# Gated cross attention with a stream mixer: low parts a unit later on GpSimd, ScalarE's free work ahead of its bank copies, other units for two projections

## The reference

```python
# step 1: windowed cross attention; q and k from the normalised x, v from the context
q = Wq @ xn + bq;  k = Wk @ xn + bk;  val = Wv @ ctx + bv          # 256 x 2048 a batch
# windows of 128 columns, 8 heads of 32 rows
attn = softmax(q_h^T k_h / sqrt(32), masked);  o = gelu(attn applied to val)
x = x + tanh(g_xattn) * (Wo @ o + bo) * mask
# step 2: four streams of 512 columns, mixed row by row
xn2 = layernorm(x)
H_res = sinkhorn(50 iterations, 4 x 4 logits of each row);  H_pre, H_post = softmaxes
y = (sum_n H_pre[n] * stream_n) @ W_branch
out_i = sum_j ((1-g) I + g H_res)[i, j] * stream_j + H_post[i] * y
x = x + tanh(g_ffn) * out
```

## Time and profile before

| what | value |
|---|---|
| median of three runs | 1883.52 us (1878.68 to 1887.21) |
| profiled execution | 1878.06 us, span 1876.2 us |
| granted TensorE clock, mean | 0.884 |
| busy: TensorE, VectorE, ScalarE, GpSimd | 1423.7, 1390.8, 1055.6, 799.5 us |

### The profile page before, as it was taken

One profiled execution on the slowest core, in us unless ns is written; L12 is line 12 of the kernel. 1 busy time (PEld: TensorE's weight loads), 2 busy tenths in 40 slices (PEclk: granted clock), 3 DMA queues, 4 the chain that ended last, 5 costly groups with the idle time before them and its releaser, 6 DMA issues.

```text
span 1876.2 us, 35394 instructions
## 1 busy us (share of the span) xinstructions
PE 1423.7 (76%) x12448; PEld 859.5 (46%) x12448; DVE 1390.8 (74%) x3582; ACT 1055.6 (56%) x2017; POOL 799.5 (43%) x1333
## 2 busy tenths in 40 slices
PE   2779999888988888888888888888898886522223
PEld 1546556555645454545555454445555554220011
DVE  3334545666788897888888888888777887777777
ACT  3457776666766666665666666656666564311111
POOL 3223334555454544455354535454454534323320
PEclk9889999999989998999899898989999997755656
DMA  8457766566656665666656565665556543321123
GB/s 259 138 163 194 215 172 167 170 179 194 180 149 179 182 190 168 197 186 186 195 157 176 171 181 165 187 167 171 170 167 175 136 125 90 101 79 56 56 87 115
DMA packets 173920, 299.85 MB, mean 160 GB/s; under 512 B 23568, under 2 KB 74640, under 8 KB 169648
## 3 DMA queue, kind: packets, MB, share of 16 engines
q1 hardware_dynamic: 156336, 264.03, 45.0%
q0 software_dynamic: 17408, 33.56, 10.2%
HBM read 179.81 MB, written 67.11 MB: 132 GB/s over the span
## 4 chain that ended last, share of the span: by engine, by line
PE 43%; DVE 22%; POOL 11%; ACT 10%; issue 9%; DMA 2%; SPq 2%; DVEq 0%; POOLq 0%; ACTq 0%
PE pr L610 11%; PE pr L624 7%; PE pr L637 6%; POOL kp L536 5%; PE f L739 4%; DVE ssum L1160 4%; PE av_ps L724 4%; POOL ctx_hl L476 3%; DVE otile_odd L1207 3%; DVE negm L1034 2%; PE av_ps L728 2%; SPq L404 2%; DVE sa L1161 2%; PE s_ps L697 2%; DVE sv L1161 1%
## 5 line engine op out<-in xcount | busy, mean ns | idle before, releaser
L1160 DVE TENSOR_REDUCE ssum<-kp 128x16 f32<-128x64 f32 x768 | 181.8, 237 | 208.3 <-POOL kp L536 206.1
L536 POOL TENSOR_TENSOR kp<-ke,sa 128x64 f32<-128x64 f32 x392 | 158.0, 403 | 283.8 <-DVE sa L1161 283.8
L536 POOL TENSOR_TENSOR kp<-ke,sv 128x64 f32<-128x64 f32 x376 | 166.2, 442 | 226.7 <-DVE sv L1161 225.7
L476 POOL TENSOR_TENSOR ctx_hl<-ctx_raw,ctx_hl 128x512 bf16<-128x512 f32 x128 | 149.6, 1174 | 217.3 <-ACT ctx_hl L792 217.3
L610 PE MATMUL pr<-x_hl,wq 128*128 128x512 bf16 x768 | 205.8, 426 | 35.1 <-POOL x_hl L471 35.1
L1034 DVE TENSOR_REDUCE negm<-s_ps 128x4 bf16<-128x512 f32 x256 | 167.0, 652 | 74.7 <-PE s_ps L697 73.2
L697 PE MATMUL s_ps<-k_st,q_st 97*128 97x128 bf16 x1024 | 104.4, 226 | 151.3 <-DVE negm L1034 138.4
L610 PE MATMUL pr<-x_hl,wk 128*128 128x512 bf16 x768 | 197.4, 412 | 8.0 <-DVE logit L1100 8.0
L637 PE MATMUL pr<-o_sb,wo 128*128 128x512 bf16 x768 | 188.0, 389 | 8.8 <-POOL o_sb L482 6.6
L837 ACT ACTIVATE probs<-st_ps,key_bias 128x512 f32<-128x512 f32 x256 | 173.3, 677 | 30.0 <-PE st_ps L711 29.5
L471 POOL TENSOR_TENSOR x_hl<-xc,x_hl 128x512 bf16<-128x512 f32 x128 | 148.5, 1160 | 92.8 <-ACT x_hl L805 92.8
(11 more groups left out here) (140 smaller groups left out, 2965.0 us busy)
## 6 DMA issues: line engine op xcount, KB each, us to landing
xs<-in_dram SPq DMA_DIRECT2D x128, 256.0 KB, 4.9
xc<-in_dram SPq DMA_DIRECT2D x32, 1024.0 KB, 10.7
ctx_raw<-in_dram SPq DMA_DIRECT2D x32, 1024.0 KB, 7.0
x1c<-in_dram POOLq DMA_DIRECT2D x64, 512.0 KB, 9.3
x_dram<-x1c SPq DMA_DIRECT2D x32, 1024.0 KB, 4.7
q_st<-q_hl SPq DMA_DIRECT2D x384, 64.0 KB
k_st<-k_hl SPq DMA_DIRECT2D x384, 64.0 KB
x1t_even<-x_dram SPq DMA_DIRECT2D x16, 1024.0 KB, 5.8
```

Of the source, the lines that this page charges most:

```text
L476: ins = nc.gpsimd.tensor_tensor(ctx_hl[:, 1, t, :], ctx_raw[:, t, :], ctx_hl[:, 0, t, :], ALU.subtract)
L536: nc.gpsimd.tensor_tensor(kp[:], ke[:], v, ALU.mult).then_inc(kp_made, 1)
L1160: cf.link(nc.vector.tensor_reduce(s_t, k, AX.X, ALU.add))
```

## The change

The tables move work between the units of a chunk. Of x, the low parts move from units 2, 5, 6, 7 to 3, 5, 6, 7, while the high parts stay at 1, 4, 5, 6. Of the context, the low parts move from units 0, 1, 1, 4 to 1, 2, 2, 3, and the high parts stay at 0, 0, 1, 1. The first half of the value projection moves from unit 6 to 4, the output projection from units 4 and 5 to 5 and 6, the mixer's logits from 7 to 5, its selection from 8 to 9, and its statistics from 1 and 3 to 2 and 5. All output tiles stand one unit later (`TILE_AT` 54 for 53), the transposes of their `pre` part two units later. The second `add_x` of a chunk moves from unit 7 to unit 0 of the next, the store of the sum from unit 1 to 2.

On GpSimd the two kinds of low part change places within a unit: the context's now stands between scalings 1 and 2, x's between 2 and 3. On ScalarE the context's and x's high parts, the first product and the first of the output tiles move from behind the bank copies and the reciprocal to the place ahead of them. `spare` gets three columns, one for each use.

```diff
--- before.py
+++ after.py
@@ -53,11 +53,11 @@
 FIRST = -2 * UPC
 RING = 4
 
-HI_X_AT, LOW_X_AT = [1, 4, 5, 6], [2, 5, 6, 7]
-HI_CTX_AT, LOW_CTX_AT = [0, 0, 1, 1], [0, 1, 1, 4]
-
-T_AT, LOGITS_AT, SELECT_AT = [3, 3, 4, 4], 7, 8
-STAT_B_AT = [1, 3]
+HI_X_AT, LOW_X_AT = [1, 4, 5, 6], [3, 5, 6, 7]
+HI_CTX_AT, LOW_CTX_AT = [0, 0, 1, 1], [1, 2, 2, 3]
+
+T_AT, LOGITS_AT, SELECT_AT = [3, 3, 4, 4], 5, 9
+STAT_B_AT = [2, 5]
 
 
 STAT_AT = UPC + STAT_B_AT[1]
@@ -67,15 +67,15 @@
 SINK += [(it, it + 1) for it in range(RETURN + 1, ITERS, 2)]
 RETURN_AT = SINK_AT + SINK.index((RETURN, None))
 
-BESIDE = dict(load=-8, first=-6, xpre=-5, pre=-4, branch_0=0, branch_1=1, out_0=-1, out_1=0,
+BESIDE = dict(load=-8, first=-6, xpre=-5, pre=-3, branch_0=0, branch_1=1, out_0=-1, out_1=0,
               stream_1=0, stream_2=1, y=2, stream_3=4, pair_1=5, pair_2=6, pair_3=7, store_0=5, store_1=8)
 BEHIND = dict(load=-5, first=-3, xpre=-3, pre=-2, branch_0=-1, branch_1=-1, out_0=-1, out_1=0,
               stream_1=0, stream_2=1, y=2, stream_3=3, pair_1=3, pair_2=4, pair_3=5, store_0=4, store_1=6)
 LAST_BESIDE = B - 3
-TILE_AT = {(f, t): UNITS * (f + 1) + 53 + UPC * t for f in range(LAST_BESIDE + 1) for t in range(DT)}
+TILE_AT = {(f, t): UNITS * (f + 1) + 54 + UPC * t for f in range(LAST_BESIDE + 1) for t in range(DT)}
 TILE_AT.update({(B - 2, t): NU + SINK_AT - 1 + 6 * t for t in range(DT)})
 TILE_AT.update({(B - 1, t): NU + SINK_AT + len(SINK) + 1 + 6 * t for t in range(DT)})
-assert SINK_AT + len(SINK) < 53
+assert SINK_AT + len(SINK) < 54
 LAST = TILE_AT[B - 1, DT - 1] + UPC
 XS = DT * 4
 XSN = 4
@@ -116,7 +116,7 @@
 
     if b == 1:
         return [p - 1 for p in range(XS)]
-    return [UNITS * (b - 1) + UPC * (p // 4 - 2) + 2 * (p % 4) for p in range(XS)]
+    return [UNITS * (b - 1) + UPC * (p // 4 - 2) + (1, 3, 4, 5)[p % 4] for p in range(XS)]
 
 
 STAT_PIECES = {}
@@ -134,9 +134,9 @@
     made += [("pre", f, t) for f, t in tiles_at(g, "pre")]
     if 0 <= G + 1 < NG:
         made += {0: [("q", G + 1, 0)], 1: [("q", G + 1, 1)], 2: [("k", G + 1, 0)], 3: [("k", G + 1, 1)],
-                 6: [("v", G + 1, 0)], 7: [("v", G + 1, 1)]}.get(r, [])
-    if 0 <= G - 1 < NG and r in (4, 5):
-        made += [("o", G - 1, 2 * (r - 4)), ("o", G - 1, 2 * (r - 4) + 1)]
+                 4: [("v", G + 1, 0)], 7: [("v", G + 1, 1)]}.get(r, [])
+    if 0 <= G - 1 < NG and r in (5, 6):
+        made += [("o", G - 1, 2 * (r - 5)), ("o", G - 1, 2 * (r - 5) + 1)]
     if g == -1:
         made.append(("csum", 0, 0))
     return made
@@ -218,7 +218,7 @@
         gate_sb = sb("gate_sb", [P, 3])
         gt = sb("gt", [P, 8])
         ones = sb("ones", [P, P])
-        spare = sb("spare", [P, 1])
+        spare = sb("spare", [P, 3])
         csum = sb("csum", [P, NL])
         bn_a = sb("bn_a", [P, DT, 4, 6])
         mv_a = sb("mv_a", [P, DT, 2])
@@ -433,7 +433,7 @@
                 if r == 0 and 1 <= G + 2 < NG:
                     sp.wait_ge(x_split, DT * (G + 2))
                     load_xc(G + 2)
-                if r == 1 and 0 <= G - 2 < NG:
+                if r == 2 and 0 <= G - 2 < NG:
                     store_x1(G - 2)
                 for later in STAT_PIECES.get(g + 4, []):
                     load_xs(*later)
@@ -557,18 +557,20 @@
                     for ready in ffn_at(g, STAT_AT + 1 + part):
                         stat_b(ready, part)
                 scale_at(f, its, 1)
+                for H, t in at_step(g, -1, LOW_CTX_AT):
+                    split_ctx(H, t)
+                if 0 <= G - 1 < NG and r == 4:
+                    low_gelu(G - 1, 0)
+                scale_at(f, its, 2)
+                if 0 <= G - 1 < NG and r == 4:
+                    low_gelu(G - 1, 1)
                 for H, t in at_step(g, -2, LOW_X_AT):
                     split_x(H, t)
-                if 0 <= G - 1 < NG and r == 3:
-                    low_gelu(G - 1, 0)
-                scale_at(f, its, 2)
-                if 0 <= G - 1 < NG and r == 3:
-                    low_gelu(G - 1, 1)
-                for H, t in at_step(g, -1, LOW_CTX_AT):
-                    split_ctx(H, t)
                 scale_at(f, its, 3)
-                if 0 <= G - 1 < NG and r in (6, 7):
-                    add_x(G - 1, r - 6)
+                if 0 <= G - 1 < NG and r == 7:
+                    add_x(G - 1, 0)
+                if 0 <= G - 2 < NG and r == 0:
+                    add_x(G - 2, 1)
 
         @block.tensor
         def _(pe):
@@ -948,6 +950,17 @@
                     exp_scores(g - 1)
                 if 0 <= G - 1 < NG and r == 3:
                     hi_gelu(G - 1)
+
+                for H, t in at_step(g, -1, HI_CTX_AT):
+                    hi_ctx(H, t)
+                for H, t in at_step(g, -2, HI_X_AT):
+                    norm_x(H, t)
+                    hi_x(H, t)
+                for done, t in tiles_at(g, "first"):
+                    first_products(done, t)
+                for pair in range(2):
+                    for done, t in tiles_at(g, f"out_{pair}"):
+                        first_out(done, t, pair)
                 made = banked_at(g)
                 for n, what in enumerate(made):
                     if what[0] in "qk":
@@ -964,11 +977,6 @@
                         inverse_den(g - 2)
                 if not made and 0 <= g - 2 < NU:
                     inverse_den(g - 2)
-                for H, t in at_step(g, -1, HI_CTX_AT):
-                    hi_ctx(H, t)
-                for H, t in at_step(g, -2, HI_X_AT):
-                    norm_x(H, t)
-                    hi_x(H, t)
                 if g == FIRST + UPC + 3:
                     w_parts(2, wv, wv_loaded)
                 if g == -2:
@@ -977,11 +985,6 @@
                     gelu(G - 1)
                 if g >= 0 and u == 15 and b + 1 < B:
                     xstat(b + 1)
-                for done, t in tiles_at(g, "first"):
-                    first_products(done, t)
-                for pair in range(2):
-                    for done, t in tiles_at(g, f"out_{pair}"):
-                        first_out(done, t, pair)
                 for n in range(2):
                     for ready in ffn_at(g, STAT_AT + 1 + n):
                         inverse_roots(ready, n)
@@ -1071,7 +1074,7 @@
                     cf.link(ins)
 
             def stat_finish(f):
-                nc.vector.memset(spare[:, 0:1], 0.0)
+                nc.vector.memset(spare[:, 1:2], 0.0)
                 for t in range(DT):
                     ins = nc.vector.bn_aggr(mv_b[:, t, :], bn_b[:, t].rearrange("p j s -> p (j s)"))
                 ins.then_inc(mv_b_ready, 1)
@@ -1161,7 +1164,7 @@
                 nc.vector.reciprocal((sv if half else sa)[:], s_t).then_inc(scale_made, 1)
                 if half and it == RETURN:
                     dve.wait_ge(scale_made, HALVES * f + 2 * it)
-                    ask(nc.vector.memset(spare[:, 0:1], 0.0))
+                    ask(nc.vector.memset(spare[:, 2:3], 0.0))
                 if half and it == ITERS - 1:
                     dve.wait_ge(scale_made, HALVES * (f + 1))
                     coefficients(f)
```

## The result

| what | before | after |
|---|---|---|
| median | 1880.32 us (1877.19 to 1887.21) | 1899.14 us (1894.87 to 1901.76) |
| span of the profiled execution | 1876.2 us | 1900.0 us |
| granted clock, mean | 0.884 | 0.871 |

The ratio is 1.0103 with an interval of 1.0082 to 1.0123: the change made the kernel slower by 19 us, where 1839 was forecast, and outside the stated range of 1795 to 1890. The forecast put 0.12 on slower. (The two profiled executions differ by 23.8 us; the changed one is the slowest of its five.)

The account below looks back on a forecast made before the run. VectorE was taken to set the period, held by GpSimd's scaling. -4.5 + 1.2 + 0.6 + 0.3 = -2.4 us a chunk, -50 over 21 chunks, -45 with the tail: 1833, median 1839, range 1795 to 1890.

Parts of the forecast that it names:

- The removed term in unit 1: VectorE's 3.24 us idle for GpSimd's scaling in unit 1 goes, leaving that unit at about 6.5 us.
- The added term in unit 2: Two context low parts on GpSimd between scalings 1 and 2 make VectorE wait 1.2 us a chunk.
- All of GpSimd's terms together: VectorE's waits for scaling, a chunk: 4.05 us removed, 1.2 added in unit 2, 0.6 in units 6 and 7.
- The tail: After the attention, the last two batches' Sinkhorn iterations start one unit later: +5.2 us.
- What it moves on TensorE: Moved transposes, projections and branch products keep TensorE's sum per chunk; with 3.3 us of slack left, nothing counted.
- ScalarE's order only a price (0.3 us a chunk): ScalarE's free work ahead of q's copy and the reciprocal may wait for `xc`'s load: 0 to 0.6 us, 0.3 taken.
- Rival 1: TensorE becomes the bound through slow projections in units 3 to 7, costing VectorE 1.2 us a chunk: median 1863, chance 0.15.
- Rival 2: VectorE's additions stretch beside x's low parts on GpSimd, 2.1 us a chunk instead of 0.6: median 1870, chance 0.15.
- The sign "TensorE's wait for the maximum nearly halved and the clock higher": Listed as showing the forecast right: TensorE waits nearly half as long for VectorE's maximum, and the clock rises.
- Rival 3: `xc`'s load lands after 15.2 us, ScalarE holds q and the reciprocal, VectorE loses 4.2 us: median 1927, chance 0.12.
- Rival 4: The added waits hide and only the removed 4.5 us a chunk shows: median 1794, chance 0.13.
- The early chunks: The ten chunks before 497.8 us have few additions and no such idle time; no change counted.

Follow-up runs that it names:

- kernel 4: Kernel before with GpSimd's new order of low parts and ScalarE's new order of free work, projections and mixer units unmoved: 1819.67 us, ratio 0.9668.
- Experiment 8: Changed kernel with GpSimd waiting for the mixing coefficients, and the transposes of `pre` in unit 2 instead of 3: 1856.80 us, ratio 0.9891.
- 11: Transposes of `pre` in unit 2 instead of 3, on both orders plus moved mixer units and GpSimd's wait for the coefficients: 1873.66 us, ratio 0.9945.
- Kernel 3: Kernel before with only ScalarE's order changed, its context and x copies, first products and first output tiles ahead of the bank copies: 1809.23 us, ratio 0.9612.
- kernel 2: Kernel before with only GpSimd's part changed, the units and order of the low parts of context and x: 1836.11 us, ratio 0.9758.
- experiment 1: Changed kernel plus one wait: where a batch's iterations end, GpSimd waits until VectorE has made the mixing coefficients: 1874.05 us, ratio 0.9961.

## Why the prediction was wrong

**What was right.** The removed term in unit 1: it fell to 5.97 us, against "about 6.5". The added term in unit 2: VectorE waited 1.30 us there (1.2 taken). A timeline of the changed kernel:

```profile
1216.35 2.72 POOL L476 TENSOR_TENSOR ctx_hl<-ctx_raw,ctx_hl 128x512 bf16<-128x512 f32 x2
...
1219.36 0.22 DVE L1163 TENSOR_REDUCE ssum<-kp 128x16 f32<-128x64 f32 x1 [1.30 <-POOL kp L536]
```

All of GpSimd's terms together (-4.05 + 1.2 + 0.6 = -2.25 us a chunk) measured (43.1 - 69.1) / 12 = -2.2. That close a sum is partly luck. By units, the mean wait for the scaling fell by 2.8 us in unit 1 (3.24 forecast) but rose from 0.89 to 1.14 in unit 0, where 0.81 should have gone; it rose by 0.9 in unit 2 (1.2), which as a whole grew by 2.5 us where about 1 was expected, and by 0.3 in units 6 and 7 together (0.6), and fell by 0.5 in unit 3, where nothing was counted. The 0.4 us for the copy of q did not go: 5.1 us in three batches became 5.6, now in unit 2. The tail: from the last maximum to the end 300.4 us against 296.0, +4.4 (5.2 forecast).

**The step that failed** is "What it moves on TensorE": "The sum per chunk is the same", and "so I count nothing here either". With it fails the silence on the mixer's moved units, for which the sum has the tail alone, 5 us. The order inside a chunk has a price that a sum of work does not show. On kernel 4, the price of the projections measured 26 us (46 for the values, 20 back), that of the mixer's units 38 us and 30 more for the burst. Added to the orders' -61 (1819.67 against about 1881) this gives 1820 + 26 + 68 = 1914 us, 15 above what was measured (21 by the ratios). So the parts are not additive, as experiments 8 and 11 show too: with the mixer's units already moved, the projections cost 11 us (1899.14 against 1887.73, which also differ in one statistic). For the orders alone the measured 1820 lies in the forecast's own range, 1812 to 1863, and is more than the -45 I had for the whole. (The lower end of that range is not what its terms' ends add up to: without any added wait they give -4.5 us a chunk, not -3.6.)

**The cover I misread.** I laid the gain at the low parts' later units and gave ScalarE's order only a price (0.3 us a chunk). Kernel 3 shows the reverse: -72 us by ScalarE's order without any low part moved. The earlier trace rows held it: the copy of the context stood behind a copy of q that waited 3.75 us. Both edits act on that one place, and either shortens unit 1 (10.16 us a chunk to 7.13 in kernel 2, 6.77 in kernel 3, 6.44 with both), so their gains do not add.

**Rival 1** (TensorE the bound, 1863) came in part. TensorE was not the bound: its busy time in the stretch did not grow (529.7 to 507.1 us, with one in eighty of its records missing after), and its wait for the maximum rose. But what the rival described, little to do ahead of unit 3 and then slow work, is in the trace. Unit 2 of the chunk shown had a clock of 0.65, and in unit 3 TensorE came to k only behind its wait and two sets of transposes:

```profile
1222.68 0.61 PE L699 MATMUL s_ps<-k_st,q_st 97*128 97x128 bf16 x4 [4.09 <-DVE negm L1037]
...
1224.34 1.12 PE L659 MATMUL pr<-id_sb,x1c 128*128 128x128 f32 x4
1225.25 1.06 PE L686 MATMUL pr<-id_sb,xpre 128*128 128x128 f32 x4
```

ScalarE's wait for the projection of k, in the stretch before and after:

```profile
ACT k_hl L819 <- PE pr L610: 22.5, 12, 3.2
```

```profile
ACT k_hl L821 <- PE pr L612: 47.7, 24, 3.0
```

VectorE's wait for the copy of k grew by 13.3 us, 1.1 a chunk, where the rival had 1.2. Experiment 8, which takes the second set out of unit 3, halves it. The sign "TensorE's wait for the maximum nearly halved and the clock higher" failed: the wait grew by half, and the clock of the stretch went from 0.92 to 0.91 (kernel 4: 0.96).

**Rival 2** (exclusion beside the additions, 1870) has the right mechanism and the wrong place and size. Additions took 7.4 us more in 12 chunks, 0.6 a chunk, where the rival had 1.5 above the forecast; the large part was one product at the end of the iterations. In the changed kernel the additions (two inputs in SBUF) took 0.69 to 0.71 us on average where no low part of GpSimd overlapped them, and 1.11 to 1.17 where one did. The low halves of q and k (one of two inputs in a PSUM bank) took 0.74 us, and the iterations' sums (one input) 0.24, either way. The Trainium skill states an exclusion for this pair, an instruction of VectorE with two inputs in SBUF and one of GpSimd that reads SBUF, on the page "SBUF — State Buffer", section "Who interferes with whom", and the trace agrees. That the hold lasts over five queued instructions of GpSimd is this trace's; the page speaks of one instruction.

**Rival 3** (head of line on `xc`, 1927) had the right sign, and the time by another cause: no wait for `xc` stands in the changed kernel's three batches. In kernels 3 and 4 the wait is there, 16.9 and 7.9 us, and did not keep them from being the fast ones. What ScalarE's order may cost is elsewhere: the first maximum comes 4.5 us later, and in the first two batches VectorE waits 62.9 us for the reciprocal (44.2 before).

**Rival 4** (only the removal shows, 1794) is refuted for the change, and is near to what its ScalarE part does alone.

**The early chunks**, counted as nothing, cost 1.7 us in the first eight; but the attention starts 4.5 us later, which no term had. In kernel 3 it starts 5.0 us later, in kernel 2 1.6, so most of this is ScalarE's order.

**What stays open.** Where the 38 us of the mixer's units arise is shown for the three batches, mostly as a wait for GpSimd's scaling, but not which of the moved operations makes them; the pieces of the next batch's statistics were never moved alone. Why moving the output projection gives back 14 to 20 of the values' 46 us was not told apart. ScalarE's order was tested as one edit of three blocks: the rows point to the copy of the context in unit 1, but no run moves that alone. That moving low parts on top of ScalarE's order costs 10 us is seen only as a longer wait for the scaling (34.3 against 29.5 us).

## What to carry to other kernels

When an engine's written order holds work that waits for nobody behind work that waits for another engine, move the free work ahead first, and time that alone. An unchanged sum does not make a move between units free: for each moved instruction ask what stands right behind it on its engine, and who waits for that. Where a change takes waits out of a helper engine, look at the places where that engine now has nothing to wait for (the end of an iteration, a pause). Its queued work can run there in one piece, as the five low parts did here, and hold up an operation of another engine on which everything waits.

## What the runs showed of the hardware that I had not expected

A VectorE product of 128x64 with two inputs in SBUF took 5.65 us instead of 0.23 beside five back-to-back subtractions of GpSimd (records of 1.6 us each, their starts 1.1 us apart). It began behind the start of the first and ended with the last, so it got no turn between them. With a wait of GpSimd for the coefficients made from that product ahead of the five (experiment 1) it took 0.225 us.
